# Offset convolutions of the 3x3 and 5x5 branches: from fp32 matmuls to pairs of fp16 matmuls with stacked weights

## The reference, cut to what matters

```python
def deform_block(x, ow, ob, dw, pw, pb, K):
    pad = K // 2
    offsets = conv2d(x, ow, ob, pad)               # 128 channels -> 2*K*K
    out = deform_depthwise(x, offsets, dw, K, pad) # bilinear samples, one pair of offsets per tap
    return conv2d(out, pw, pb, 0)
```

## Time and profile before

| | |
|---|---|
| median of three runs | 7678.86 us |
| the profiled execution | 7680.1 us, its span 7678.3 us |
| mean granted TensorE clock | 0.941 of full speed |
| TensorE busy | 6834.0 us, 89% of the span |
| VectorE busy | 4948.2 us, 64% |
| ScalarE busy | 3981.9 us, 52% |
| GpSimd busy | 765.5 us, 10% |
| offset convolutions, all three branches (L1627) | 2928 records, 1349.8 us busy |
| of them 3x3 and 5x5 | 360 and 1000 records |

### The profile page before, as it was taken

One profiled execution on the slowest core, in us unless ns is written; L12 is line 12 of the kernel. 1 busy time (PEld: TensorE's weight loads), 2 busy tenths in 40 slices (PEclk: granted clock), 3 DMA queues, 4 the chain that ended last, 5 costly groups with the idle time before them and its releaser, 6 DMA issues. The chain is left out here.

```text
span 7678.3 us, 129559 instructions
## 1 busy us (share of the span) xinstructions
PE 6834.0 (89%) x49546; PEld 4426.1 (58%) x49546; DVE 4948.2 (64%) x10049; ACT 3981.9 (52%) x5490; POOL 765.5 (10%) x542
## 2 busy tenths in 40 slices
PE   5999999999996898998989989899898977997998
PEld 2555555555552455775567745677556664554787
DVE  6877877787782477786777867777677772333012
ACT  3656656665661356775567745677557761111000
POOL 1211111111121101001010010100101000000000
PEclk9999999999998899998999989999999988998778
DMA  3000000000001344444444444444444431011466
GB/s 115 16 31 32 15 24 31 16 24 31 24 15 62 88 115 112 107 107 108 103 113 108 96 118 106 114 107 95 119 107 112 108 94 56 33 49 60 104 157 185
DMA packets 181412, 617.72 MB, mean 80 GB/s; under 512 B 54985, under 2 KB 63617, under 8 KB 138035
## 3 DMA queue, kind: packets, MB, share of 16 engines
q1 hardware_dynamic: 180707, 608.45, 31.4%
HBM read 542.23 MB, written 65.59 MB: 79 GB/s over the span
## 5 line engine op out<-in xcount | busy, mean ns | idle before, releaser
L2118 PE MATMUL b_p<-m_S,b_hkt 64*128 64x144 f32 (+37 forms) x27520 | 2062.9, 304 | 281.3 <-DVE b_acc L2000 145.3
L2118 PEld LDWEIGHTS b_p<-m_S,b_hkt 64*128 64x128 f32 x27520 | 1927.8, 191 | 524.6 <-issue 230.9
L2067 DVE TENSOR_TENSOR m_S<-m_rx,m_ry 128x140 f32<-128x140 f32 (+26 forms) x5312 | 1576.4, 346 | 516.4 <-PE b_p L2118 328.6
L1627 PE MATMUL b_p<-b_hp,b_ow 128*98 128x512 f32 (+2 forms) x2928 | 1349.8, 612 | 49.1 <-POOL b_hp L1620 49.1
L1972 ACT ACTIVATE m_rx<-m_pp,b_mcol 128x512 f32<-128x512 f32 (+6 forms) x1328 | 765.0, 648 | 1027.8 <-DVE m_S L2067 1025.9
L533 ACT ACTIVATE a_ex<-a_p_t 128x1024 f32<-128x1024 f32 x526 | 538.4, 1024 | 712.2 <-PE a_p_t L465 710.1
L1627 PEld LDWEIGHTS b_p<-b_hp,b_ow 128*98 128x98 f32 (+2 forms) x2928 | 405.8, 144 | 854.8 <-issue 848.2
L597 DVE TENSOR_REDUCE a_nm<-a_p_x 128x1 f16<-128x1024 f32 x537 | 658.1, 1226 | 284.0 <-PE a_p_x L454 267.9
L1976 ACT ACTIVATE m_ry<-m_pp,b_mrow 128x544 f32<-128x544 f32 (+6 forms) x1328 | 762.5, 646 | 0.0
L2000 DVE SCALAR_TENSOR_TENSOR b_acc<-b_p,b_dwc,b_acc 128x323 f32<-128x323 f32 (+14 forms) x1088 | 622.9, 575 | 191.9 <-PE b_p L2118 191.8
L603 DVE TENSOR_TENSOR a_el<-a_ex,a_eh 128x1024 f16<-128x1024 f32 x525 | 693.7, 1321 | 3.6
(11 more groups left out here) (175 smaller groups left out, 6511.1 us busy)
## 6 DMA issues: line engine op xcount, KB each, us to landing
m_pp<-sampling_positions SPq DMA_DIRECT2D x664, 512.0 KB, 6.5
d_win<-merged_kernels SPq DMA_DIRECT2D x192, 263.0 KB, 5.2
b_xin<-x SPq DMA_DIRECT2D x23, 1024.0 KB, 8.5
b_xr<-x SPq DMA_DIRECT2D x15, 1024.0 KB, 13.6
x<-b_xr SPq DMA_DIRECT2D x15, 1024.0 KB, 4.3
a_xh<-in_x SPq DMA_DIRECT2D x9, 1536.0 KB, 6.4
a_xr<-in_x SPq DMA_DIRECT2D x9, 1536.0 KB, 6.4
x<-a_xr SPq DMA_DIRECT2D x9, 1536.0 KB, 5.3
```

Of the source, the lines that this page charges most:

```text
L1627: last = e.matmul(bank_of(u[1])[0:M, :].rearrange("p (a b) -> p a b", b=W), ow[:, OW0[gj] + k * M:OW0[gj] + (k + 1) * M], hp[:, s, n * 16 ...
L2067: e.tensor_tensor(S[:, k % NS, 0:(r1 - r0) * w].rearrange("p (a b) -> p a b", b=w), rx[:, u, xo[cc]:xo[cc + 1]].rearrange("p (a b) -> p a ...
L2118: last = e.matmul(G[:, a0 - top:z0 - top, c0 - left:c1 - left], hkt[64 * s:64 * s + 64, SIDE * cr + cc, :], S[64 * s:64 * s + 64, k % NS, ...
```

## The change

The offset convolutions of K = 3 and K = 5 no longer run in fp32. Both operands are split into two fp16 halves whose sum is the fp32 value.

- **Weights.** `ows` holds for each tap the high halves as columns 0 to 2K²-1 and the low halves, scaled by 2048, as columns from `LO_ROW` (32 or 64) on. One matmul has 50 or 114 columns of weights in place of 18 or 50, and the results of the low halves land in other PSUM partitions of the same bank. Columns between are zero. VectorE builds `ows` once, in the block of constants, from a new input `b_ows`.
- **Image.** `hs` is `hp` seen as fp16 pairs: each 4-byte word has the high half at t = 0 and the low half at t = 1. A matmul reads one of them, so its moving operand steps over every second fp16 element. There are two matmuls per tap, t = 0 and 1, in place of one fp32 matmul.
- **Taking offsets.** `take_offsets` adds the bias to the high rows as before, waits for itself, and then a new `scalar_tensor_tensor` adds the low rows times 1/2048. The bank is free after the second one.
- **Padding.** `xin` is normalised in place first (`normalise_pair`), then `pad_stacked` casts it into t = 0 and subtracts to get t = 1: six instructions where `pad` had two. In the stage of 7 all this is GpSimd's; `chunk` becomes plain copies of the normalised `xin` there. In the opening it is VectorE's, the padding for K = 7 included, and GpSimd keeps only `chunk_normalised` and `add_grid`.
- `CONV_GAP` is 56 in place of 32.

```diff
-CONV_GAP = 32
+CONV_GAP = 56
+LO_ROW = {3: 32, 5: 64}
+LO_UP = 2048.0
+def stacked_cols(K):
+    return LO_ROW[K] + 2 * K * K
+def stacked_at(K):
+    return sum(k * k * stacked_cols(k) for k in KS if k < K)
...
+        hs = hp[:].bitcast(F16).rearrange("p s a (b t) -> p s a b t", t=2)
...
-            last = e.matmul(bank_of(u[1])[0:M, :].rearrange("p (a b) -> p a b", b=W), ow[:, OW0[gj] + k * M:OW0[gj] + (k + 1) * M],
-                            hp[:, s, n * 16 + dy + far:n * 16 + dy + far + 16, dx + far:dx + far + W], start=(k == 0), stop=(k == K * K - 1))
+            r0, c0 = n * 16 + dy + far, dx + far
+            if K in LO_ROW:
+                M = stacked_cols(K)
+                into = bank_of(u[1])[0:M, :].rearrange("p (a b) -> p a b", b=W)
+                for t in range(2):
+                    last = e.matmul(into, ows[:, stacked_at(K) + k * M:stacked_at(K) + (k + 1) * M], hs[:, s, r0:r0 + 16, c0:c0 + W, t],
+                                    start=(k == 0 and t == 0), stop=(k == K * K - 1 and t == 1))
...
+            if KS[gj] in LO_ROW:
+                lo = LO_ROW[KS[gj]]
+                e.tensor_scalar(off[0:M, r, :], bank_of(u[1])[0:M, :], ob[0:M, gj:gj + 1], None, ALU.add).then_inc(s_off.sem, 1)
+                e.wait_ge(s_off.sem, s_off.at(low_q + 1))
...
+                e.scalar_tensor_tensor(off[0:M, r, :], bank_of(u[1])[lo:lo + M, :], 1.0 / LO_UP, off[0:M, r, :], ALU.mult, ALU.add).then_inc(s_cu[u[1]].sem, 1)
...
+        def normalise_pair(e, g, gns, loads, done):
+            e.wait_ge(s_x.sem, s_x.at(loads * 16))
+            e.sem_inc(sh["tick"], 1)
+            for s in range(2):
+                norm_of(e, xin[:, s, :], xin[:, s, :], gns[g][s]).then_inc(s_hs.sem, 1)
+            e.wait_ge(s_hs.sem, s_hs.at(done + 2))
+            e.sem_inc(sh["tick"], 1)
+
+        def pad_stacked(e, done):
+
+            for s in range(2):
+                e.tensor_copy(hs[:, s, RM:RM + H, RM:RM + W, 0], xin[:, s, :].rearrange("p (a b) -> p a b", a=H)).then_inc(s_hs.sem, 1)
+            for s in range(2):
+                e.wait_ge(s_hs.sem, s_hs.at(done + 3 + s))
+                e.sem_inc(sh["tick"], 1)
+                e.tensor_tensor(hs[:, s, RM:RM + H, RM:RM + W, 1], xin[:, s, :].rearrange("p (a b) -> p a b", a=H),
+                                hs[:, s, RM:RM + H, RM:RM + W, 0], ALU.subtract).then_inc(s_hp.sem, 1)
+
+        def chunk_normalised(e):
+            for s in range(2):
+                for r in range(SIDE):
+                    last = e.tensor_copy(h8[:, SIDE * r:SIDE * r + SIDE, s, :, :].rearrange("p c i j -> p i c j"),
+                                         xin[:, s, r * CH * W:(r + 1) * CH * W].rearrange("p (i c j) -> p i c j", i=CH, c=SIDE))
+            last.then_inc(s_h8.sem, 1)
...
             @block.gpsimd
             def _(e):
+                e.wait_ge(s_hs.sem, s_hs.at(2))
+                chunk_normalised(e)
+                for c, (gj, unit) in enumerate(firsts):
+                    add_grid(e, gj, unit, c, c % 2)
+
+            @block.vector
+            def _(e):
                 gns = [[sh["gn"][:, g, s, :] for s in range(2)] for g in range(G3)]
-                pad(e, 0, gns, 1)
-                chunk(e, 0, gns, 1)
+                normalise_pair(e, 0, gns, 1, 0)
+                pad_stacked(e, 0)
                 for c, (gj, unit) in enumerate(firsts):
+                    if (gj, unit) == (0, 2):
+                        normalise_pair(e, 1, gns, 2, 4)
                     if unit == 3:
                         filled(e, first[c])
-                        pad(e, gj + 1, gns, gj + 2)
-                    add_grid(e, gj, unit, c, c % 2)
...
+                        if gj == 0:
+                            pad_stacked(e, 4)
+                        else:
+                            pad(e, 2, gns, 3)
+                    take_offsets(e, gj, unit, first[c], c // 2, c % 2, c)
...
                         if g == 2:
-                            pad(e, 0, gns, loads + 1)
+                            normalise_pair(e, 0, gns, loads + 1, pr * 8 + 8)
+                            pad_stacked(e, pr * 8 + 8)
...
-                        chunk(e, (1, 2, 0)[g], gns, loads + 1)
+                        if g == 2:
+                            chunk_normalised(e)
+                        else:
+                            chunk(e, (1, 2)[g], gns, loads + 1)
                         for c, (gj, unit) in enumerate(convs):
+                            if g == 2 and (gj, unit) == (0, 2):
+                                normalise_pair(e, 1, gns, loads + 2, pr * 8 + 12)
                             if g == 2 and unit == 3:
                                 filled(e, conv_u[c])
                                 e.sem_inc(sh["tick"], 1)
-                                pad(e, gj + 1, gns, loads + gj + 2)
+                                if gj == 0:
+                                    pad_stacked(e, pr * 8 + 12)
+                                else:
+                                    pad(e, 2, gns, loads + 3)
                             add_grid(e, gj, unit, q_of(c), ring_of(c)[1])
```

More of the change, by code:

```diff
@@ L1552, in layer1 @@
     PW = W + 2 * RM
-    OW0 = [sum(2 * K ** 4 for K in KS[:g]) for g in range(G3 + 1)]
+    NW = [2 * K ** 4 for K in KS]
     posd = [nc.dram_tensor(f"sampling_positions{g}", [2, M7, N], F32).ap() for g in range(G3)]
@@ L1570, in layer1 @@
         f2 = a.sb("f2", [HID, G3, P])
-        ow = a.sb("ow", [P, OW0[G3]])
+        ow = a.sb("ow", [P, NW[2]])
+        ows = a.sb("ows", [P, stacked_at(KS[2])], F16)
         grid = a.sb("grid", [M7, N])
@@ L1626, in conv_matmul, with take_offsets @@
             dy, dx = divmod(k, K)
-            last = e.matmul(bank_of(u[1])[0:M, :].rearrange("p (a b) -> p a b", b=W), ow[:, OW0[gj] + k * M:OW0[gj] + (k + 1) * M],
-                            hp[:, s, n * 16 + dy + far:n * 16 + dy + far + 16, dx + far:dx + far + W], start=(k == 0), stop=(k == K * K - 1))
+            r0, c0 = n * 16 + dy + far, dx + far
[6 more added lines that the diff above has]
+            else:
+                last = e.matmul(bank_of(u[1])[0:M, :].rearrange("p (a b) -> p a b", b=W), ow[:, k * M:(k + 1) * M],
+                                hp[:, s, r0:r0 + 16, c0:c0 + W], start=(k == 0), stop=(k == K * K - 1))
             if k == K * K - 1:
                 last.then_inc(s_pu.sem, 1)
-        def take_offsets(e, gj, unit, u, uses, r):
+        def take_offsets(e, gj, unit, u, uses, r, low_q=0):
             M = 2 * KS[gj] ** 2
@@ L1786, in layer1 @@
             zt = ai.sb("zt", [P, PADT, P])
+            wf = ai.sb("wf", [P, NW[0] + NW[1]])
             @block.sync
@@ L1811, in _ @@
                 e.memset(pool[:], 0.0)
-                e.wait_ge(s_i.sem, s_i.at(16 * 14))
+                e.wait_ge(s_i.sem, s_i.at(16 * 15))
                 e.tensor_tensor(ob[:], ob[:], base[:], ALU.add)
+                e.memset(ows[:], 0.0).then_inc(s_is.sem, 1)
+                e.wait_ge(s_is.sem, s_is.at(1))
+                for g, K in enumerate(KS[0:2]):
+                    M = 2 * K * K
+                    w = wf[:, sum(NW[:g]):sum(NW[:g + 1])].rearrange("p (k m) -> p k m", m=M)
+                    both = ows[:, stacked_at(K):stacked_at(KS[g + 1])].rearrange("p (k m) -> p k m", m=stacked_cols(K))
+                    e.tensor_copy(both[:, :, 0:M], w).then_inc(s_is.sem, 1)
+                    e.wait_ge(s_is.sem, s_is.at(2 + 2 * g))
+                    e.tensor_tensor(w, w, both[:, :, 0:M], ALU.subtract).then_inc(s_is.sem, 1)
+                    e.wait_ge(s_is.sem, s_is.at(3 + 2 * g))
+                    e.tensor_scalar(both[:, :, LO_ROW[K]:LO_ROW[K] + M], w, LO_UP, None, ALU.mult)
         a.open()
@@ L1843, in _ @@
             def _(e):
+                gns = [[sh["gn"][:, g, s, :] for s in range(2)] for g in range(G3)]
+                normalise_pair(e, 0, gns, 1, 0)
+                pad_stacked(e, 0)
                 for c, (gj, unit) in enumerate(firsts):
-                    take_offsets(e, gj, unit, first[c], c // 2, c % 2)
+                    if (gj, unit) == (0, 2):
+                        normalise_pair(e, 1, gns, 2, 4)
+                    if unit == 3:
+                        filled(e, first[c])
+                        if gj == 0:
[3 more added lines that the diff above has]
+                    take_offsets(e, gj, unit, first[c], c // 2, c % 2, c)
                     if unit == 3:
@@ L2245, in laid_out @@
     t["b_grid"] = grid.reshape(M7, N)
-    t["b_ow"] = np.concatenate(ows, 1)
+    t["b_ow"] = ows[2]
+    t["b_ows"] = np.concatenate(ows[0:2], 1)
     t["b_base"] = base
```

19 lines of the change are left out of this document (10 added, 9 removed).

## The result

The changed kernel takes 7490.7 us (7483.1 to 7494.5) against 7679.7 in the same job, a ratio of 0.9752 (95% interval 0.9740 to 0.9764). It is faster by 189 us, where 268 were forecast; the time lies 6 us above the range. The profiled execution took 7483.1 us, its span is 7481.2.

What follows compares the result with a forecast made beforehand. TensorE was taken to bound the convolution stretches, VectorE and ScalarE the taps without convolutions. The opening's -64 and four stages of -51 sum to -268, from the median 7411 us; range 7370 to 7485, chance of the forecast 0.76.

Steps and rivals of the forecast that it cites:

- TensorE bounds the stretch, VectorE has a margin: In the K = 7 stages' 5x5 stretch TensorE stays the bound, 9.1 us a tap; VectorE's margin falls to 0.9 us.
- 8.83 us a tap: TensorE's need in the 5x5 stretch: 6.84 us of its own work plus 1.99 of convolutions at the new price.
- Rival 1: VectorE and ScalarE become the bound in the whole convolution stretch, 9.7 us a tap: 7479 us, chance 0.13.
- Rivals 2 and 3: The convolutions' fp16 pairs cost what fp32 did, 7670 us, chance 0.07; or every-second-element reads are slower, 7962 us, chance 0.04.
- I take 0.217, since rows 7 have the same type and width, and only the step differs: Price of each fp16 convolution matmul, taken from profiled fp16 matmuls of 512 columns: 0.217 us, bounds 0.217 to 0.4355.
- Three more for GpSimd: In each K = 7 stage, 3 us added because longer GpSimd padding meets VectorE's tap marks.
- 7.8 in the gap (3.5 taps, 27 us): Between 3x3 and 5x5 convolutions in a K = 7 stage, taps take 7.8 us each, 27 us in all.
- GpSimd itself is late for nobody: In the K = 7 stages, GpSimd's padding, 5 to 25 us, ends within the 27 us before the first 5x5 matmul.
- The opening, -64: Opening: convolutions -59.4, start -2, wait before 5x5 -4, end -3, added +4; about -64 us (-54 to -70).
- the two slots of `off`: In the opening, waiting for one of two slots to come back adds 4 us, bounds 0 to 10.
- the -2 at the start: At the opening's start, 7.6 us of GpSimd padding becomes 6 us of VectorE instructions: minus 2 us.
- A stage, -51 (bounds -59 to -40): Each of four K = 7 stages: stretch from 351 to 297 us, -54, plus 3 for GpSimd.

Runs made afterwards that it cites:

- run 7: Kernel of run 6 with only the matmuls of the image's high half, the low half's left out: 7344.6 us, 0.9561 of the kernel before.
- run 1: Changed kernel with the two fp16 halves of the padded image in separate planes, so matmuls read neighbouring elements: 7459.6 us, 0.9711 of the kernel before.
- run 4: Kernel of run 1 with the stage's padding casting and subtracting one image row instead of 32, good for its time alone: 7425.5 us, 0.9665.
- run 2: Changed kernel, packed layout, with GpSimd's casts and subtractions of the stages' padding in eight pieces of four rows: 7467.8 us, 0.9725.
- 11: Kernel of run 1 with eight more GpSimd subtractions a stage, written to a buffer nobody reads: 7505.9 us, 0.9777.
- run 5: Changed kernel with both separate planes and the stage's padding in eight pieces of four rows: 7436.2 us, 0.9680.
- run 6: Kernel of run 5 with the stage's normalisations of both pairs also in eight pieces of 128 elements: 7431.2 us, 0.9673.

## Why the prediction was off

- **TensorE bounds the stretch, VectorE has a margin:** right beside the 5x5, where TensorE is 99% busy. That its 197.5 us are the 198 of the forecast is partly luck: the 8.83 us a tap that I had worked out missed what the step adds (4.6 x 2 x 0.037 = 0.34), and the 9.1 that I took held 0.27 without a term behind it. Rival 1 (VectorE at 19 of 20, TensorE under 92%) is not what the profile shows, though its 7479 lies nearest to the time; run 7 shows that bound further down. Rivals 2 and 3 did not occur.
- **"I take 0.217, since rows 7 have the same type and width, and only the step differs":** this step failed. The step costs: 0.254 a record (12.7 us for 50), and 0.224 with neighbours. Planes gave back 31 us. The value lay inside my bounds, but its share was not carried into the range of each stage, and at 1360 records the 0.033 us between 0.25 and 0.217 are 45 us of TensorE time. The Trainium skill (SBUF — State Buffer, the part on ports) has two accesses to a 16-byte line as enough for full bandwidth. The matmuls of the changed kernel and of run 1 differ in nothing but the step, and run 1 is 12% faster a record; the measurement decides.
- **"Three more for GpSimd":** mis-sized, in the stages the largest miss. The padding costs 8.5 us a stage (run 4), 34 in all by the medians, instead of 12. I counted only the wait of one tap mark and neither that every item beside such an instruction is held for its whole length (2.4 instead of 0.4 us), nor what follows: TensorE starves, and its stretch at half clock is 15 us and more where run 4 has 10. The Trainium skill (GPSIMD Engine Reference, 1. Specifications) names the shared interface for VectorE instructions with two SBUF inputs, and runs 2, 4 and 11 agree: 23, 34 and 46 us. I had cited the rule and priced it by its weakest row.
- **"7.8 in the gap (3.5 taps, 27 us)":** this failed too, and the runs with short padding show by how much: the gap takes 32 us in them (55 items in 32.3 us in run 4, 9.4 us a tap), 37.6 in the changed kernel. I had the 7.8 from taps at full clock where VectorE and ScalarE are the bound; in the gap TensorE is granted half clock for 10 us even in run 4. But run 2 takes 32.0 us for its gap at full clock, so the slow clock alone does not make the 5 us a stage; what does is not tested. The window of run 2's gap:

```profile
3067.00:3099.00 32.00, 27.45 (x355) 24.30 (x354) 30.73 (x72) 24.95 (x32) 15.16 (x33) 1.00 0.58 145
```

- **"GpSimd itself is late for nobody":** right. No wait of TensorE for GpSimd stands at the first 5x5 matmul, not even with the gap of 32.
- **The opening, -64:** -57.7 (143.8 to 86.2, and the start as long as before). The step of 2 elements accounts for about 9 of TensorE there (272 records), of which planes gave back 7: this is the 6 that the opening is short of, and more, since the 4 us that I had added for the two slots of `off` did not come. The 5x5 wait of 4.6 and the end of 9.5 us (from 2489.7 to 2499.2) are as forecast; the -2 at the start did not come: from GpSimd's first memset to the first matmul it is 39.8 us as before, since the block of constants is 1 us longer.
- **A stage, -51 (bounds -59 to -40):** -32.0, -34.0, -31.1 and -32.1 by the tap marks, 129 in all instead of 204, outside the bounds. In the first stage the stretch gave 39.2, the items behind the last convolution took 1.7 more, and the head before the first convolution, 46.3 us before, became 51.8 (2943.2 to 2995.0), which I had costed at nothing, because I looked there only for GpSimd being late and not for whom it holds. GpSimd works 20 us there as before, but 7.7 of them are now casts and subtractions; with those down to one row the head is 46.3 us again (run 4).

The first stage in parts, in us, from the tap marks and the starts of the convolutions:

| | head | 3x3 | gap | 5x5 | behind | stage |
|---|---|---|---|---|---|---|
| before | 46.3 | 87.0 | 19.0 | 244.5 | 110.0 | 506.8 |
| forecast | 46 | 72 | 27 | 198 | 110 | 456, with 3 for GpSimd |
| changed kernel | 51.8 | 76.3 | 37.6 | 197.5 | 111.7 | 474.8 |
| planes (run 1) | 50.7 | 74.1 | 37.1 | 191.9 | 114.9 | 468.8 |
| planes, one row (run 4) | 46.3 | 74.1 | 32.3 | 191.9 | 114.3 | 458.9 |
| planes, pieces (run 5) | 49.8 | 74.1 | 32.1 | 190.9 | 114.4 | 461.4 |

The sum: the four stages lack 75 us of the forecast and the opening 6; 2 of these came back where the edit changes nothing. Of the 75, the step is 22 (run 1) and the padding beyond the 12 I had allowed 25 (37.5, run 4). The remaining 28 are 7 a stage; in the first stage of run 4 they are 6: the gap makes 5 of them (32 instead of 27), the items behind the last convolution 4 (114 instead of 110), the 3x3 part 2, and the 5x5 part takes 6 back (192 instead of 198). The pace of neighbours, 0.224 for 0.217, is 2 a stage in this. What makes the items behind slower stays open, and so does the cause of the gap's 5; run 6 shows no gain from cutting up the long normalisations of GpSimd (8.7 us a pair).

**A better version:** kernel 5, 7436.2 us, beats the changed kernel by 54 and the kernel before by 242.

## What to carry to other kernels

When a step is moved to GpSimd, or grows there, ask not only whether it is late, but which VectorE instructions with two SBUF operands run beside it and who lives off them: cut GpSimd's instructions so short that one wait is harmless, even if their sum grows. Lay 16-bit operands of a matmul out so that neighbours are read. And where a margin between two engines is under 10% of the period, a saving on the first may be worth only part of itself, here two thirds (run 7); put that into the range.

## What the runs showed of the hardware

- fp16 moving operands of 512 columns at a step of two elements: 0.25 us a record, at step one 0.22; with TensorE at half clock 0.43 in both, so the step costs nothing at half clock (2413.37 to 2413.80 in the first, 2413.50 to 2413.93 in the second):

```profile
2413.37 0.16 PEld L1646 LDWEIGHTS b_p<-b_hp,b_ows 128*50 128x50 f16 x1 [0.26 <-issue]
2413.80 0.17 PEld L1646 LDWEIGHTS b_p<-b_hp,b_ows 128*50 128x50 f16 x1 [0.26 <-issue]
```
```profile
2413.50 0.17 PEld L1647 LDWEIGHTS b_p<-b_hsp,b_ows 128*50 128x50 f16 x1 [0.26 <-issue]
2413.93 0.17 PEld L1647 LDWEIGHTS b_p<-b_hsp,b_ows 128*50 128x50 f16 x1 [0.26 <-issue]
```

- A VectorE instruction with both inputs in SBUF waits out a GpSimd instruction of this kind whole (2.13 us for 90 elements), and gets its turn between two of them.
- A cast of 1024 elements on GpSimd takes 1.5 us into every second element and 1.1 us into neighbours (4 a stage: 6.1 and 4.4 us busy).
- Some 5 us in which TensorE waited in pieces of 1 to 1.7 us were followed by 15 us at half clock; in run 4 a stretch with TensorE busy for 7.7 of 9 us was followed by 10. Over the first stage of K = 7 the mean granted clock fell from 0.97 to 0.94 with the change, which this document does not price:

```profile
3001.00:3508.00 507.00, 473.34 (x5004) 362.48 (x5004) 389.03 (x974) 377.11 (x505) 45.70 (x23) 0.97 0.48 110
```
```profile
2943.00:3418.00 475.00, 436.43 (x5004) 375.25 (x5005) 405.49 (x982) 377.38 (x505) 56.63 (x32) 0.94 0.51 119
```
